# Head attention on one core: the product with the values moves to the second half of the next key tile

## The chip, the cores and the metric

One core of a Trainium2 chip runs the whole program in one launch. The metric is the device time of that launch in microseconds (us). The engines are TensorE (PE, with its weight loads listed as PEld), VectorE (DVE), ScalarE (ACT), GpSimd (POOL) and SyncE (SP, which issues most DMAs). Three runs of the kernel before took 1535.26, 1531.8 and 1535.34 us; the median is 1535.26.

## The reference, cut to what matters

Two layers, each an attention and a feed-forward part, over x (8 sequences x 256 x 512) and a context of the same shape. The first attention is the part that the change touches. It has 16 heads of 16 rows each; both axes of its score matrix, queries t and keys s, have 512 places:

```python
q = jnp.einsum('oc,bct->bot', Wq, target) + bq[None, :, None]
k = jnp.einsum('oc,bcs->bos', Wk, source) + bk[None, :, None]
v = jnp.einsum('oc,bcs->bos', Wv, source) + bv[None, :, None]
dot = jnp.einsum('bhdt,bhds->bhts', q, k) / math.sqrt(HEAD_DIM)
dot = mask * dot - (1.0 - mask) * NEG
amap = jax.nn.softmax(dot, axis=-1) * mask
out = jnp.einsum('bhts,bhds->bhdt', amap, v)      # heads joined again
x = x + out                                       # target was layernorm(x)
```

The rest (a feed-forward part whose weights are quantised and restored, a second attention with one head, a second feed-forward part with ternary weights) comes after it and isn't changed.

## The kernel before, in words

The program first restores quantised weights, then runs the head attention for 8 sequences (`head_attention_block`), then the dense rest. The head attention is a pipeline whose order is written out by hand, one queue for each engine; semaphores tie the queues together.

A sequence b is split into 4 groups g of 4 heads, a group into 4 key tiles c of 128 keys. A tile (g, c) has two halves of two heads. The scores are computed twice. `row_scores` (line 828, TensorE) has the queries on the partitions; VectorE takes each row's maximum from it (`maxima`, line 1162), 16 blocks for a group, ahead of the group's turn. `column_scores` (line 837) has the keys on the partitions and the maximum already subtracted, through three extra rows of the stacked operand Qs. ScalarE takes its exponential (`exps`, line 920) into `prob`. Row scores use three PSUM banks in turn (pA), column scores three others (pB): a row matmul waits until the maximum of the third one before it is taken, a column matmul until the exponential of the third one before it is taken.

`values` (line 847, TensorE) multiplies `prob` of one key tile with the values of four heads, four products of 32 columns beside each other, and adds up over the 4 key tiles in the bank pV. It waits for the last exponential of its tile, and for its first tile of a group also until pV has been read. `av_evac` (line 925, ScalarE) copies pV to U. Before the change `values` of a tile stands behind the first half of the next tile, and `av_evac` behind the first two exponentials of tile (g, 0).

Between them the table `MISC` puts side jobs, all of which use the single bank pM, so that each waits until the one before has been read. For a tile it names a job behind the first and one behind the second half: q and k of the next sequence (line 782; in (0,0) and (1,0), q in the first half, k in the second), v of the next sequence (line 788; two in (2,3)), nm, which turns the split row maxima of the next group (line 801; first half of (g,1)), t, which turns U back (line 795; first half of (g,2)), and o, which turns the finished sequence before (line 817; two in (0,3)). Where a job and `values` stand in the same half, `values` is first.

Their readers: ScalarE reads q and k (`q_evac`, line 903) and nm (`nm_evac`, line 913); GpSimd then splits q and k into three bfloat16 parts (`split`, from line 990) and issues the DMA that puts the maxima into Qs (`max_rows`, line 1022). VectorE reads t (`normalise`, lines 1191 to 1198, behind the first two maxima of (g, 2)), v (line 1183) and o (`residual`, line 1207), which adds the input x that SyncE has loaded to xres (line 716). VectorE also splits the maxima (`max_parts`, lines 1170 to 1176, behind the last maxima of (g, 0)), takes statistics for the normalised input (`ln_stats`, behind (1,3)), a peak of the context (behind (2,1)) and applies the normalisation (`ln_apply`, line 1148, behind (3,2)).

SyncE stores the parts of q and k to memory and fills the stacks Qs and Ks from there (`fill`, lines 688 to 695), each group once the column matmuls that read it are through; the fill of group 3 is the last thing that it does for a sequence, and the load of xres is the first of the next.

The row matmuls that run beside the columns of a tile belong to a group ahead: in tile (g, 0) the last four blocks of group g + 1, in the other tiles the first twelve of group g + 2. In the last sequence there are no q, k and v jobs, and the row matmuls end with tile (2,0).

Of the kernel before, what the change touches and what calls it, by code (L numbers as in the profile page):

```python
# [59 lines left out]
def wait(eng, sem, value):  # L60

    if isinstance(value, int) and value <= 0:
        return
    eng.wait_ge(sem, value)
# [433 lines left out]
def head_attention_block(nc, keep, dram, A):  # L498
# [3 lines left out]
    with ExitStack() as ctx:  # L502
# [115 lines left out]
        def present(job, first, last):  # L618
            return job is not None and not (job[2] < 0 and first) and not (job[2] > 0 and last)

        def row_units(b, g, c):

            ahead = g + 1 if c == 0 else g + 2
            nb, ng = (b, ahead) if ahead < NG else (b + 1, ahead - NG)
            return nb, ng, 12 if c == 0 else 4 * (c - 1), ahead >= NG
# [11 lines left out]
        def over_sequences(body):  # L637
            for b in range(B):
                body(b, b == 0, b == B - 1, b >= B - 2)
# [111 lines left out]
        def _(pe):  # L751
# [69 lines left out]
            def row_scores(b, g, u):  # L821

                if u == 0:
                    pe.wait_ge(filled[g], FILL * (b + 1))
                n = 64 * b + 16 * g + u
                wait(pe, s["max_done"], n - 2)
                j, tt = u // 4, u % 4
                nc.tensor.matmul(pA[n % 3], Qs[0:MAX_ROW, g, j, P * tt:P * (tt + 1)], Ks[0:MAX_ROW, g, j, :],  # L828
                                 start=True, stop=True).then_inc(s["a_pe"], 1)

            def column_scores(b, g, c, j):

                if c == 0 and j == 0:
                    pe.wait_ge(maxrow[g], 16 * (b + 1))
                n = 64 * b + 16 * g + 4 * c + j
                wait(pe, s["exp_done"], n - 2)
                nc.tensor.matmul(pB[n % 3], Ks[:, g, j, P * c:P * (c + 1)], Qs[:, g, j, :],  # L837
                                 start=True, stop=True).then_inc(s["b_pe"], 1)

            def values(b, g, c):  # L840

                pe.wait_ge(s["exp_done"], 64 * b + 16 * g + 4 * c + 4)
                if c == 0:
                    wait(pe, s["av_act"], 4 * b + g)
                    pe.wait_ge(s["vt_ready"], 4 * b + g + 1)
                for j in range(G):
                    x = nc.tensor.matmul(pV[32 * j:32 * (j + 1), :], vt[:, g % 2, c, j, :], prob[:, c, j, :],  # L847
                                         start=(c == 0), stop=(c == DK - 1))
                x.then_inc(s["av_pe"], 1)
# [15 lines left out]
            def body(b, first, last, ending):  # L865
                for g in range(NG):
                    for c in range(DK):

                        nb, ng, u0, next_one = row_units(b, g, c)
                        jobs = MISC.get((g, c), [None, None])  # L870
                        for half in range(2):
                            for j in (2 * half, 2 * half + 1):
                                column_scores(b, g, c, j)
                                if not (last and next_one):
                                    row_scores(nb, ng, u0 + j)
                            if half == 0:
                                if c:
                                    values(b, g, c - 1)
                                elif g:
                                    values(b, g - 1, DK - 1)  # L880
                                elif not first:
                                    values(b - 1, NG - 1, DK - 1)
                            if present(jobs[half], first, last):
                                kind, i, ahead = jobs[half]
                                run(kind, i, b + ahead)
                            if last and (g, c) in LAST and LAST[g, c][half]:
                                run(*LAST[g, c][half])

            over_sequences(body)
            values(B - 1, NG - 1, DK - 1)  # L890
            run("t", 3, B - 1)
# [3 lines left out]
        @block.scalar  # L895
        def _(act):
            def q_evac(b, i, which=(0, 1)):
                for n in which:
                    act.wait_ge(s["q_pe"], 4 * b + 2 * i + n + 1)
                    if n == 0:  # L900
                        act.wait_ge(s["bias"], 1)
                    wait(act, s["q_pool"], 4 * b + 2 * i + n - 1)
                    nc.scalar.activation(qf[n][:], pM[:], ACT.Identity, bias=(bq4 if n == 0 else bk)[:, i:i + 1],  # L903
                                         scale=0.25 if n == 0 else 1.0).then_inc(s["q_act"], 1)

            def nm_evac(b, g):
                act.wait_ge(s["nm_pe"], 4 * b + g + 1)

                if g >= 2:
                    act.wait_ge(maxrow[g - 2], 16 * (b + 1))  # L910
                else:
                    wait(act, maxrow[g + 2], 16 * b)
                nc.scalar.activation(nrow[g % 2][:], pM[0:3 * G, :], ACT.Copy).then_inc(s["nm_act"], 1)

            def exps(b, g, c, half):
                for j in (2 * half, 2 * half + 1):
                    act.wait_ge(s["b_pe"], 64 * b + 16 * g + 4 * c + j + 1)
                    if j == 0:
                        wait(act, s["av_pe"], 16 * b + 4 * (g - 1) + c + 1)
                    nc.scalar.activation(prob[:, c, j, :], pB[(64 * b + 16 * g + 4 * c + j) % 3], ACT.Exp).then_inc(s["exp_done"], 1)  # L920

            def av_evac(b, g):
                act.wait_ge(s["av_pe"], 16 * b + 4 * g + 4)
                wait(act, s["t_pe"], 4 * b + g)
                nc.scalar.activation(U[:], pV[:], ACT.Copy).then_inc(s["av_act"], 1)

            for u in W["scalar"](act):
                if u - 1 in FIRST and FIRST[u - 1][0] in "qk":
                    kind, i, _ = FIRST[u - 1]
                    q_evac(0, i, ("qk".index(kind),))  # L930

            act.wait_ge(W["d_used"], W["d_steps"])
            act.wait_ge(W["a_used"], W["a_steps"])
            nm_evac(0, 0)

            def body(b, first, last, ending):
                for g in range(NG):
                    for c in range(DK):
                        exps(b, g, c, 0)
                        if c == 0:  # L940
                            if g:
                                av_evac(b, g - 1)
                            elif not first:
                                av_evac(b - 1, NG - 1)
                            if g < 2 and not last:
                                q_evac(b + 1, g, (0,))
                        if c == 1:
                            if g < NG - 1:
                                nm_evac(b, g + 1)
                            elif not last:  # L950
                                nm_evac(b + 1, 0)
                        exps(b, g, c, 1)
                        if c == 0 and g < 2 and not last:
                            q_evac(b + 1, g, (1,))
                        if last and (g, c) == (3, 0):
                            act.wait_ge(s["x_turned"], 1)
                            nc.scalar.activation(xh.rearrange("p k t -> p (k t)"), turned2.rearrange("p a b -> p (a b)"),
                                                 ACT.Copy, scale=XS).then_inc(s["x_high"], 1)

            over_sequences(body)  # L960
            av_evac(B - 1, NG - 1)

# [1078 lines left out]
```

## Time and profile before

| | us |
|---|---|
| median of three runs | 1535.26 |
| the profiled execution, its own time | 1524.93 |
| its span | 1523.1 |
| TensorE busy in it | 1390.8 |
| VectorE busy in it | 1031.6 |
| ScalarE busy in it | 592.7 |
| GpSimd busy in it | 276.1 |

Profile numbers come from the one profiled execution, not from the three runs. Busy shares are averages over stages with different limits. A matmul's listed duration contains the time to drain the array, so neighbouring matmuls overlap in the listing; the step from one start to the next says how fast they are issued.

### The profile page before, as it was taken

What the parts mean: (1) busy time and instruction counts of PE and PEld (TensorE: products, weight loads), DVE (VectorE), ACT (ScalarE), POOL (GpSimd) and SP (SyncE); (2) the same over time, 40 slices, a digit from 0 to 9 for tenths busy, and PEclk for the clock granted to TensorE, in tenths of its full rate; (3) what the DMA queues carried; (4) which work ended last, traced back from release to release, by engine and by line L of the source; (5) the groups of instructions that cost most, each with busy time, mean ns of one, the idle gap of its engine ahead of it and who ended that gap; (6) DMA issues with size and microseconds to landing.
All of it is one profiled execution on the core that took longest, in us unless ns stands there. A gap on an engine that the chain in (4) does not pass through costs nothing.

```text
span 1523.1 us, 23289 instructions
## 1 busy us (share of the span) xinstructions
PE 1390.8 (91%) x8981; PEld 811.0 (53%) x9010; DVE 1031.6 (68%) x1826; ACT 592.7 (39%) x925; POOL 276.1 (18%) x495
## 2 busy tenths in 40 slices
PE   3799899899999999988898799899998999989998
PEld 1344333333333333322676577677776777767776
DVE  9987778878787887875795945654446535465353
ACT  4567366655665565555262111122111221112310
POOL 5014062533536263310000000000000000000000
PEclk9999899999999999999999999999999999999999
DMA  5012223333434333320743401000010000110000
GB/s 176 6 32 78 81 64 108 111 115 95 133 98 148 115 113 98 101 81 15 252 130 114 133 29 56 1 29 1 15 66 5 28 1 1 46 39 29 1 2 28
DMA packets 66466, 105.64 MB, mean 69 GB/s; under 512 B 13359, under 2 KB 38071, under 8 KB 66343
## 3 DMA queue, kind: packets, MB, share of 16 engines
q1 hardware_dynamic: 65335, 103.77, 21.6%
q8 instruction: 73, 1.20, 0.3%
q0 software_dynamic: 1024, 0.40, 0.1%
q14 instruction: 34, 0.28, 0.1%
HBM read 82.40 MB, written 21.35 MB: 68 GB/s over the span
## 4 chain that ended last, share of the span: by engine, by line
PE 34%; DVE 12%; DMA 4%; ACT 1%; issue 1%; POOL 0%; SPq 0%; DVEq 0%; POOLq 0%; ACTq 0%
PE double L1584 10%; PE double L1598 10%; PE double L1610 5%; PE double L1620 2%; PE double L1663 2%; PE double L1631 2%; DMA x_early<-scr_x 2%; DVE f1w L1920 1%; DMA out_x<-x_early 1%; PE double L1650 1%; DVE hid L1824 1%; DVE hv L1822 1%; DVE gate L1821 1%; PE double L1568 1%; ACT th L1708 1%
## 5 line engine op out<-in xcount | busy, mean ns | idle before, releaser
L1162 DVE TENSOR_REDUCE nmx<-level 128x1 f32<-128x512 f32 x512 | 320.1, 681 | 52.9 <-PE level L828 52.0
L920 ACT ACTIVATE prob<-level 128x512 f32<-128x512 f32 x512 | 267.7, 593 | 136.6 <-PE level L837 136.2
L828 PE MATMUL level<-Ks,Qs 105*128 105x512 bf16 x512 | 201.0, 395 | 21.3 <-DVE nmx L1162 20.1
L1708 ACT ACTIVATE th<-double 128x512 f32<-128x512 f32 x96 | 53.9, 562 | 414.1 <-PE double L1584 204.8
L837 PE MATMUL level<-Qs,Ks 108*128 108x512 bf16 x512 | 194.9, 384 | 1.0 <-ACT prob L920 0.8
L1584 PE MATMUL double<-x_parts,f0w 128*128 128x256 f16 x1408 | 157.1, 274 | 5.4 <-DVE hid L1824 2.5
L1584 PE MATMUL double<-x_parts,f1w 128*128 128x256 f16 x1408 | 155.0, 273 | 2.7 <-DVE x_parts L1809 2.7
L1584 PEld LDWEIGHTS double<-x_parts,f0w 128*128 128x128 bf16 x1408 | 137.8, 98 | 24.9 <-issue 3.9
L365 PE MATMUL level<-prob,x_parts 128*128 128x448 bf16 (+1 forms) x527 | 118.3, 378 | 33.4 <-ACT prob L317 15.2
L1584 PEld LDWEIGHTS double<-x_parts,f1w 128*128 128x128 bf16 x1408 | 137.6, 98 | 20.7 <-DVE x_parts L1809 3.1
L1770 POOL TENSOR_TENSOR rstd<-meanvar,halfpow 128x2 f32<-128x2 f32 x22 | 15.2, 691 | 725.9 <-DVE meanvar L1790 725.9
L847 PE MATMUL pV<-prob,vt 128*32 128x512 f32 x1024 | 137.2, 608 | 1.5 <-ACT prob L920 1.0
L828 PEld LDWEIGHTS level<-Ks,Qs 105*128 105x128 bf16 x512 | 50.3, 98 | 107.9 <-DVE nmx L1162 64.3
L365 PEld LDWEIGHTS level<-prob,x_parts 128*128 128x128 bf16 x540 | 53.0, 101 | 91.5 <-issue 23.9
L317 ACT ACTIVATE prob<-f1w,level_edge 128x1408 bf16<-128x1408 bf16 x60 | 85.5, 1461 | 36.9 <-PE level L365 36.8
L837 PEld LDWEIGHTS level<-Qs,Ks 108*128 108x128 bf16 x512 | 49.9, 98 | 89.2 <-ACT prob L920 37.3
L1598 PE MATMUL double<-f0w,hid 128*128 128x512 bf16 x344 | 82.1, 401 | 10.0 <-DVE hid L1824 9.7
L1598 PE MATMUL double<-f1w,hid 128*128 128x512 bf16 x344 | 75.6, 379 | 4.8 <-DVE hid L1831 4.6
L412 DVE TENSOR_SCALAR prob<-f1w 128x1408 bf16<-128x1408 bf16 x120 | 60.4, 560 | 19.5 <-PE level L365 19.2
L990 POOL TENSOR_TENSOR qf<-qf,mrow 128x512 f32<-128x512 f32 x32 | 40.5, 1266 | 151.4 <-ACT qf L903 151.4
L1598 PEld LDWEIGHTS double<-f0w,hid 128*128 128x128 f16 x352 | 35.6, 103 | 54.6 <-DVE hid L1824 9.9
L1829 DVE SCALAR_TENSOR_TENSOR gate<-th,double 128x512 f32<-128x512 f32 (+1 forms) x48 | 30.8, 642 | 42.3 <-ACT th L1708 42.3
(206 smaller groups left out, 1893.9 us busy)
## 6 DMA issues: line engine op xcount, KB each, us to landing
scr_q<-qp SPq DMA_DIRECT2D x16, 384.0 KB, 9.3
scr_k<-qp SPq DMA_DIRECT2D x16, 384.0 KB, 3.1
Qs<-scr_q SPq DMA_DIRECT2D x32, 192.0 KB
Ks<-scr_k SPq DMA_DIRECT2D x32, 192.0 KB
hid<-in_f1w1t SPq DMA_DIRECT2D x8, 704.0 KB, 5.8
hid<-in_f1w2t SPq DMA_DIRECT2D x8, 704.0 KB, 4.2
xin<-in_x SPq DMA_DIRECT2D x8, 512.0 KB, 13.2
cx<-in_ctx SPq DMA_DIRECT2D x8, 512.0 KB, 13.7
```

The source lines that it names most:

```text
L317: nc.scalar.activation(sa[:, n % RING_A, :], wn[w][:, UNIT * q:UNIT * (q + 1)], ACT.Sign, bias=edge[:, j:j + 1]).then_inc(a_made, 1)
L365: x = nc.tensor.matmul(acc[u % 2][:, c, 0:m], diag[:, level, :], tile[:, c0:c0 + m], start=(at == 0), stop=(at == len(MIX) - 1))
L412: nc.vector.tensor_scalar(sd[:, n % RING_D, :], wn[w][:, UNIT * q:UNIT * (q + 1)], FROM[ON_DVE[j]], None, ALU.is_ge).then_inc(d_made, 1)
L828: nc.tensor.matmul(pA[n % 3], Qs[0:MAX_ROW, g, j, P * tt:P * (tt + 1)], Ks[0:MAX_ROW, g, j, :], start=True, stop=True).then_inc(s["a_pe"], 1)
L837: nc.tensor.matmul(pB[n % 3], Ks[:, g, j, P * c:P * (c + 1)], Qs[:, g, j, :], start=True, stop=True).then_inc(s["b_pe"], 1)
L847: x = nc.tensor.matmul(pV[32 * j:32 * (j + 1), :], vt[:, g % 2, c, j, :], prob[:, c, j, :], start=(c == 0), stop=(c == DK - 1))
L920: nc.scalar.activation(prob[:, c, j, :], pB[(64 * b + 16 * g + 4 * c + j) % 3], ACT.Exp).then_inc(s["exp_done"], 1)
L1162: nc.vector.tensor_reduce(nmx[:, g % 2, u // 4, u % 4:u % 4 + 1], pA[(64 * b + 16 * g + u) % 3], AX.X, ALU.max, negate=True).then_inc(s["m ...
L1584: y = nc.tensor.matmul(ps_[:, e, S * n:S * (n + 1)], w[n][:, k, P * (f0 + e):P * (f0 + e + 1)], part[:, k, :], start=(k == 0 and part is x ...
L1598: y = nc.tensor.matmul(ps_[:, t, :], hid[:, r, f, P * t:P * (t + 1)], w[:, f, :], start=(f == 0 and r == 0), stop=(f == FK - 1 and r == pa ...
L1610: y = nc.tensor.matmul(ps_[:, e // 2, (e % 2) * S:(e % 2 + 1) * S], wat[kind][:, r, k, P * e:P * (e + 1)], part[:, k, :], start=(k == 0 an ...
L1708: y = nc.scalar.activation(th[:, 0:m, :], src[:, 0:m, 0:S], ACT.Tanh, scale=0.5 / XS)
```

## The change

In TensorE's queue `values` moves from behind the first half of a tile to behind the second half; it still stands ahead of a side job of the same half. In ScalarE's queue `av_evac` moves from tile (g, 0) to tile (g, 1), behind the first two exponentials there and ahead of `nm_evac`; `q_evac` of q keeps its place.

```diff
@@ tensor
-                            if half == 0:
+                            if half == 1:
                                 if c:
                                     values(b, g, c - 1)
                                 elif g:
...
@@ scalar
                         exps(b, g, c, 0)
-                        if c == 0:
+                        if c == 0 and g < 2 and not last:
+                            q_evac(b + 1, g, (0,))
+                        if c == 1:
                             if g:
                                 av_evac(b, g - 1)
                             elif not first:
                                 av_evac(b - 1, NG - 1)
-                            if g < 2 and not last:
-                                q_evac(b + 1, g, (0,))
-                        if c == 1:
                             if g < NG - 1:
                                 nm_evac(b, g + 1)
                             elif not last:
```

## Rows read from the trace of the kernel before

**Rows 1.** The page: span, TensorE's busy time, and a load's time to landing.

```profile
span 1523.1 us, 23289 instructions
...
PE 1390.8 (91%) x8981; PEld 811.0 (53%) x9010; DVE 1031.6 (68%) x1826; ACT 592.7 (39%) x925; POOL 276.1 (18%) x495
...
x_early<-scr_x SPq DMA_DIRECT2D x8, 512.0 KB, 4.0
```

**Rows 2.** Busy time by stretch: from, to, length, engines, granted clock, DMA share, GB/s.

```profile
255.67:656.23 400.56, 374.59 (x1970) 138.51 (x1968) 324.10 (x641) 239.81 (x457) 175.28 (x323) 1.00 0.36 113
390.04:456.16 66.12, 62.52 (x329) 23.06 (x328) 54.34 (x109) 40.03 (x78) 29.33 (x54) 1.00 0.38 114
674.00:680.00 6.00, 5.70 (x19) 1.93 (x20) 3.52 (x7) 2.14 (x4) 0.00 (x0) 0.50 0.23 87
```

**Rows 3.** Waits by pair, 190 to 722 us: total, times, longest.

```profile
PEld level L828 <- DVE nmx L1162: 54.7, 83, 1.4
...
DVE xres L1207 <- DMA xres<-in_x: 14.2, 7, 5.3
```

**Rows 4.** TensorE's timeline in sequence 3: start, duration, line, idle before.

```profile
389.48 0.38 PE L837 MATMUL level<-Qs,Ks 108*128 108x512 bf16 x1
...
401.92 0.66 PE L795 MATMUL pM<-identf,U 128*128 128x128 f32 x4
...
404.98 0.39 PE L828 MATMUL level<-Ks,Qs 105*128 105x512 bf16 x1 [0.87 <-DVE nmx L1162]
405.30 1.07 PE L847 MATMUL pV<-prob,vt 128*32 128x512 f32 x8
406.30 0.66 PE L817 MATMUL pM<-identf,O 128*128 128x128 f32 x4
...
407.44 0.38 PE L828 MATMUL level<-Ks,Qs 105*128 105x512 bf16 x1
408.08 0.66 PE L817 MATMUL pM<-identf,O 128*128 128x128 f32 x4 [0.26 <-DVE xres L1207]
...
410.54 1.98 PE L782 MATMUL pM<-tgt,wq 128*128 128x512 f32 x4
```

**Rows 5.** The same timeline: nm in tile (1,1); first columns of (2,3) and (3,0).

```profile
416.09 1.06 PE L847 MATMUL pV<-prob,vt 128*32 128x512 f32 x8
416.97 0.39 PE L801 MATMUL pM<-identb,nmp 128*12 128x128 bf16 x4
417.29 0.39 PE L837 MATMUL level<-Qs,Ks 108*128 108x512 bf16 x1
...
435.99 0.38 PE L837 MATMUL level<-Qs,Ks 108*128 108x512 bf16 x1
...
443.51 0.38 PE L837 MATMUL level<-Qs,Ks 108*128 108x512 bf16 x1
```

**Rows 6.** SyncE's timeline, 380 to 425 us: first refill, and the load of xres.

```profile
389.89 0.72 SPq L688 DMA_DIRECT2D Qs<-scr_q  x1
...
394.77 0.40 SPq L716 DMA_DIRECT2D xres<-in_x  x1
```

**Rows 7.** The line that loads xres: seven loads, from issue to landing.

```profile
DMA to landing us min/median/max: 12.5/13.6/14.6
```

**Rows 8.** VectorE's timeline in sequence 3.

```profile
402.62 0.26 DVE L1191 RECIPROCAL rs<-pM 128x16 f32<-128x16 f32 x1 [0.41 <-PE pM L795]
...
404.25 2.47 DVE L1162 TENSOR_REDUCE nmx<-level 128x1 f32<-128x512 f32 x4
...
407.34 0.69 DVE L1207 TENSOR_TENSOR xres<-pM,xres 128x512 f32<-128x512 f32 x1 [0.62 <-DMA xres<-in_x]
...
428.01 2.48 DVE L1162 TENSOR_REDUCE nmx<-level 128x1 f32<-128x512 f32 x4
```

**Rows 9.** ScalarE's timeline in sequence 3: the evacuation of q.

```profile
412.56 0.69 ACT L903 ACTIVATE qf<-pM,bq 128x512 f32<-128x512 f32 x1 [1.29 <-PE pM L782]
```

**Rows 10.** TensorE's timeline: the last value product of sequence 7.

```profile
714.50 1.07 PE L847 MATMUL pV<-prob,vt 128*32 128x512 f32 x8 [0.96 <-ACT prob L920]
```

## The prediction

> **What bounds the kernel now.** I read the page first: TensorE is busy 91% of a span of 1523.1 us [rows 1]. That is an average, so next came the busy times by stretch [rows 2]. The change lies in a loop of eight sequences, 192 to 716 us; sequences 1 to 6 take 400.56 us together, 66.76 each, with TensorE busy for 374.59, VectorE 324.10, ScalarE 239.81, GpSimd 175.28. What follows 720 us is untouched. Then the waits by pair [rows 3]: TensorE's weight loads before row matmuls wait 54.7 us for VectorE's maxima, and the residual addition waits 14.2 us, in 7 waits, for the load of xres.
>
> I call a column matmul c, a row matmul r, the value product V, and a tile (g,c), (0,0) opening a sequence. In the timeline of sequence 3, c and r start 0.22 us apart when nothing waits. V starts 0.31 after the r ahead of it and the next job 1.00 later: 1.09 us more than without V [rows 4]. In (0,3) the second r waits 0.87 us for a maximum and V stands right behind it; (1,3) and (2,3) have the same pattern, with 0.85 and 0.72.
>
> **One wait ties a sequence to the next.** SyncE refills Qs and Ks once the last column matmul of a sequence (c3 of (3,3), 389.48) has ended, from 389.89; only behind the eight refills, at 394.77, comes the load of xres, with 12.5/13.6/14.6 us to landing [rows 4, 6, 7]. The residual addition of (0,3) starts as it lands (407.34, 0.69 us), and the second transpose of O, o1 (408.08), waits for it [rows 4, 8]. So c3 to o1 takes 5.3 + 12.5 + 0.8 = 18.6 us here, and 5.1 + 13.6 + 0.8 = 19.5 in the mean (5.1: in sequence 1 the issue comes 4.9 after c3). TensorE alone would reach o1 after 18.3 (last r 407.44, plus 0.3, from 389.48). The period is (o1 to the next c3) + max(19.5, TensorE's way from c3 to o1). Now: 408.08 to the opening of sequence 4 at 456.16 [rows 2, 4] is 48.08, less 0.57 from c3 to the opening, 47.5; plus 19.5 is 67.0.
>
> **The change part by part.** Nothing is added or removed; 128 V and 32 evacuations of U move in their queues. I laid the new order out tile by tile with these steps: a row is readable 0.42 after r's start, a maximum occupies VectorE 0.60, r(n+3) starts 0.73 after maximum n (404.25 to 404.98), t is readable 0.70 after its start (401.92 to 402.62) [rows 4, 8].
>
> *V behind c3 r3 instead of r1.* V now gives VectorE its 1.09 us after every four r. In (1,2) the normalisation starts 1.9 after the tile's start and takes 1.63 (402.62 to 404.25), to 3.53; the tile is 3.40 long. So in (1,3) VectorE does r2, r3 of the tile before from 0.13 and 0.73; the second r waits for 0.86 instead of 0.65, the rest not at all: 3.37 us for 3.87. (2,3), from 435.99 to 443.51 = 7.52 [rows 5], becomes 4 x 0.22, 0.09 + 1.83 for v0, 4 x 0.22, 1.09, 1.83: 6.6, as its wait falls under V.
>
> *Switches.* In 12 of 16 tiles V shared its switch with the job behind it (t, nm, q, o0, v0); in four others k, o1 or v1 now follow V. A job behind an r pays up to what V pays, 0.31 - 0.22 = 0.09; nm also pays 0.10 to get back to c (0.32 for 0.22 of work), which V to nm (0.88 against 1.00) used to save [rows 4, 5]. r to t and r to nm aren't in the trace: bounds 0 and 0.19, I take 0.09 as the row nearest in kind. 8 x 0.09 + 4 x 0.10 = 1.1 us a sequence, contained in the lengths below.
> The skill speaks against the change here. In the trace the 98 ns weight loads of c and r are wholly hidden in 0.22 us steps [rows 4]. The Trainium skill, page "TensorE: Matmul & The Clock Gate", section "The mechanism", lets a weight load overlap running matmuls only where the row group differs; all of these share their rows, so the trace disagrees. By that rule every separated job would pay its load whole and the sum would lose some 0.2 us a sequence, 1.5 in all.
>
> *New waits.* (0,1), (1,1): nm comes 1.09 earlier and waits for the evacuation of k (2.0 after k's start, as 410.54 to 412.56 for q, plus 0.69 [rows 4, 9]), and V waits for that of U, which stands behind it and two exponentials: 0.1 and 0.25. With the switches 3.55 for 3.05. (1,0): o1 to q is 1.43 of work, but the second residual needs two maxima and itself after the first, 1.87: o1 to (1,1) 7.47 for 7.04. (2,0): VectorE's statistics end 2.04 after its start (in (2,0) of this sequence they end at 428.01 [rows 8]); the fourth r waits until 2.77 for its 1.53: 4.07 for 3.61. (2,1): nm, due at 0.96, waits 0.27 for the split maxima, but the backlog is gone: 3.51 for 3.69. (3,0) 2.92 for 2.85; (3,1) 3.46 for 3.23, nm 0.24 late. (3,3): normalisation and ln_apply (0.91) leave VectorE at the first row of (3,3) only 4.87 after the start of (3,2), so r3 comes at 5.60 instead of 4.93: 3.50 for 3.24. (0,0) 6.54 for 6.87. Tiles with t 3.40 for 3.33.
> On ScalarE the evacuations of U and nm are now neighbours; behind them stand two exponentials whose banks TensorE needs only 1 us later. GpSimd gets q 1.1 us sooner and then waits for nm as before; SyncE's order is the same.
>
> *The tie.* Behind the last c3 now stand r3 (waiting 0.67), V and then the opening: 2.19 us for 0.57. Refill and xres start 1.62 us earlier against the opening. TensorE's way from c3 to o1 is 2.19 + 6.54 + 3.56 + 3.40 + 3.60 = 19.3, the transfer's 19.5; as landings spread over 2.1 us, the larger of the two is 19.7 in the mean, +0.2.
>
> *Sum.* o1 to c3: 7.47 + 3.55 + 3.40 + 3.37 + 4.07 + 3.51 + 3.40 + 6.63 + 2.92 + 3.46 + 3.40 + 3.50 - 2.19 = 46.5 for 47.5; with +0.2, -0.8 a sequence. Sequences 1 to 5: -4.0. Sequence 6 has no statistics and no ln_apply: -0.6. Sequence 0 has no o: +0.4 of waits and switches, less 1.6 by c3: -1.2. Sequence 7, short of q and k, is held longest by the landing (5.3 [rows 3]); its idle stretch shrinks from 4.9 to about 3.1. After it the granted clock is 0.50, the lower level, from 674 to 680 [rows 2], and the tile there takes 5.3 for a usual 2.85; I count half of that back, -1.2. Its last six tiles have no r and go from exponential to V to exponential (V waits 0.96 for one at 714.50 [rows 10]); with V behind c3 the exponentials run under it, -0.25 a tile, -1.5. In all -8.5 us. The profiled execution (1524.93) becomes 1516.4; the median of the runs shown is 10.3 above it, 1535.26, so 1526.8.
>
> **Rivals.**
> 1. *The tie eats it: no change.* If the way from c3 to o1 is 0.6 longer than laid out (nm for k, V for U), each sequence gives back what it won; sequences 0 and 7 leave -1 to -4: 1531 to 1535. For it: 19.3 against 19.5 is a hair. Against: the waits won behind o1 don't hang on it.
> 2. *More than forecast.* If nm and q don't wait (1.2 us a sequence: 0.44 in (1,0), 0.25 twice, 0.5 in (2,1), (3,1)) and the clock stays up in sequence 7: -8.5 - 7 x 1.2 - 1.2 = -18: 1517. Against: four maxima of 0.60 outlast four pairs of 0.44.
> 3. *The landing doesn't follow its trigger: slower.* A load of the size of xres takes 4.0 us elsewhere [rows 1] and 13.6 here, behind the refills, so it should move with them. But if the traffic that holds it stays in place (stores of q and k, the x1 store), the 1.62 is lost: the gate is 21.1 after c3, 1.4 above what I count, so +0.6 a sequence, +4 in six, and sequence 7 +1.6, with its longer low clock another +1; with sequence 0 and the tail 1539. It decides once issue to landing exceeds 14.4 in the mean. Against: 12.5 to 14.6 in seven loads.
>
> **How the numbers follow.** Forecast 0.49, rival 1 0.28, rival 2 0.08, rival 3 0.15. A measurement of this kernel can't tell less than 0.3%, 4.6 us, from no change. Faster 0.57, same 0.28, slower 0.15. The forecast's own range is 1521 to 1530: switches at their bounds are 0.7 a sequence either way, the clock 1.2. For 8 in 10 I take in rival 1 and the near sides of 2 and 3: 1518 to 1538.
>
> **What would show it.** Right: the second r of (1,3) and (2,3) hardly waits; last c3 to opening grows from 0.57 to about 2.2; the waits for xres fall from 14.2 to under 9; o1 to (0,0) stays near 48.7 while the period of sequences 1 to 5 is near 66.2; (2,0) about 4.1. Wrong: issue to landing above 14.4; the 54.7 us not below 45; waits for the evacuation of U or k above 0.5 each.

## The result and the profile after

| | before | changed |
|---|---|---|
| median, us | 1534.2 (4 runs, 1531.8 to 1535.34) | 1517.76 (4 runs, 1515.08 to 1521.58) |
| ratio, 95% interval | | 0.9911 (0.9894 to 0.9928) |
| profiled execution: span | 1523.1 | 1513.3 |
| first column matmul of the loop to the first dense matmul | 529.54 | 515.59 |

The ratio makes 13.7 us (11.0 to 16.3) of 1534.2; the two medians differ by 16.4. The two profiled executions differ by less, 9.8, because the changed one reached the loop 2.8 us later (195.05 for 192.28) and spent 1.3 more behind it, both outside the change; the loop itself (from its first column matmul to the first dense matmul) is 13.95 us shorter, which agrees with the ratio. So in what follows I compare stretches inside the loop, each of one execution. The forecast was -8.5 with 1526.8 us; the measured median is 0.2 below the low end of the range, 1518.

The busy times of sequences 1 to 6 together, of sequence 3, and of a stretch of sequence 7, in the changed kernel (from, to, length, PE, PEld, DVE, ACT, POOL, granted clock, DMA share, GB/s):

```profile
258.76:647.21 388.45, 371.95 (x1973) 137.84 (x1969) 321.62 (x640) 239.55 (x456) 176.22 (x323) 1.00 0.37 116
388.54:453.33 64.79, 62.02 (x333) 22.98 (x329) 54.01 (x109) 39.93 (x76) 29.47 (x54) 1.00 0.37 116
664.20:669.50 5.30, 5.26 (x16) 2.12 (x20) 4.64 (x7) 2.39 (x4) 0.00 (x0) 0.50 0.26 99
```

Against [rows 2] the busy times hardly differ (371.95 for 374.59 on TensorE); what is gone is idle time: 388.45 us for 400.56. The low clock in sequence 7 is still there.

Its waits by pair, 190 to 712 us (total, times, longest), answering to [rows 3]:

```profile
PEld level L837 <- ACT prob L920: 65.6, 81, 1.1
...
PEld level L828 <- DVE nmx L1161: 39.0, 76, 1.6
...
PE pM L801 <- DVE nmp L1175: 5.7, 16, 0.7
...
DVE xres L1206 <- DMA xres<-in_x: 7.2, 5, 4.7
```

The wait for maxima before row matmuls, counted at their weight loads, fell from 54.7 to 39.0 (the matmuls themselves sat idle 9.6 us for 19.7), that for xres from 14.2 to 7.2, 4.7 of it in sequence 7. A new one is nm waiting for the split maxima, 5.7 us. (The wait before column weight loads grew from 37.3 to 65.6 us, but it is idle time of the weight loader; the matmuls themselves sat idle 1.1 us behind it, as the page lists.)

TensorE's timeline in sequence 3, from the last column matmul of sequence 2 (386.30) on, answering to [rows 4, 5]:

```profile
386.30 0.38 PE L837 MATMUL level<-Qs,Ks 108*128 108x512 bf16 x1
387.23 0.39 PE L828 MATMUL level<-Ks,Qs 105*128 105x512 bf16 x1 [0.55 <-DVE nmx L1161]
387.54 1.06 PE L847 MATMUL pV<-prob,vt 128*32 128x512 f32 x8
388.54 0.39 PE L837 MATMUL level<-Qs,Ks 108*128 108x512 bf16 x1
...
399.04 0.38 PE L828 MATMUL level<-Ks,Qs 105*128 105x512 bf16 x1
399.26 0.60 PE L795 MATMUL pM<-identf,U 128*128 128x128 f32 x4
399.69 0.38 PE L837 MATMUL level<-Qs,Ks 108*128 108x512 bf16 x1
...
402.43 0.39 PE L828 MATMUL level<-Ks,Qs 105*128 105x512 bf16 x1
402.65 0.60 PE L817 MATMUL pM<-identf,O 128*128 128x128 f32 x4
...
404.06 1.06 PE L847 MATMUL pV<-prob,vt 128*32 128x512 f32 x8
405.05 0.66 PE L817 MATMUL pM<-identf,O 128*128 128x128 f32 x4
...
425.17 0.39 PE L828 MATMUL level<-Ks,Qs 105*128 105x512 bf16 x1 [1.05 <-DVE nmx L1161]
...
427.15 0.38 PE L828 MATMUL level<-Ks,Qs 105*128 105x512 bf16 x1
427.88 0.38 PE L801 MATMUL pM<-identb,nmp 128*12 128x128 bf16 x4 [0.35 <-DVE nmp L1175]
428.20 0.39 PE L837 MATMUL level<-Qs,Ks 108*128 108x512 bf16 x1
```

What to see: the second r of (0,3) comes at 402.43, 0.1 late, where 0.87 stood. From the last c3 to the opening are 2.24 us. t starts 0.22 behind an r, the same step as between any two matmuls, and c follows 0.43 later. In (2,0) the fourth row waits 1.05, and nm of (2,1) 0.35. The xres loads of the changed kernel, issue to landing, for [rows 7]:

```profile
DMA to landing us min/median/max: 12.6/13.1/14.2
```

I put the start of c3, of the load of xres, its landing, and of o1 of every sequence beside each other. Means of sequences 1 to 5, us:

| | before | changed | forecast |
|---|---|---|---|
| o1 to the next last column matmul (c3) | 47.51 | 46.05 | 46.5 |
| c3 to the issue of xres | 5.01 | 5.02 | 5.1 |
| issue to landing | 13.73 | 13.34 | 13.6 |
| landing to o1 | 0.77 | 0.78 | 0.8 |
| c3 to o1 | 19.51 | 19.14 | 19.7 |
| sum, the period | 67.02 | 65.19 | 66.2 |

Median tile lengths of sequences 1 to 5, groups (g) down, before and changed: (0,c) 6.87 3.05 3.33 6.22 and 6.38 3.45 3.28 4.01; (1,c) 6.54 3.05 3.33 3.87 and 6.90 3.45 3.29 3.26; (2,c) 3.61 3.69 3.33 7.52 and 4.07 3.69 3.28 6.40; (3,c) 2.85 3.23 3.33 3.24 and 2.93 3.69 3.28 3.56.

### The profile page after: what moved, and what is told of

It is laid out like the page before. It is cut to its first block, busy times and chain, and to the rows that moved or that the text cites. A ratio compares the mean times of both kernels' runs of the same rounds, so it can differ in the third digit from the quotient of the medians.

```text
span 1513.3 us, 23289 instructions
## 1 busy us (share of the span) xinstructions
PE 1392.0 (92%) x8981; PEld 812.7 (54%) x9010; DVE 1030.0 (68%) x1826; ACT 592.8 (39%) x925; POOL 277.2 (18%) x495
## 4 chain that ended last, share of the span: by engine, by line
PE 34%; DVE 12%; DMA 3%; ACT 2%; issue 1%; POOL 1%; SPq 0%; DVEq 0%; POOLq 0%; ACTq 0%
PE double L1583 11%; PE double L1597 10%; PE double L1609 5%; PE double L1662 2%; PE double L1619 2%; PE double L1630 2%; DMA x_early<-scr_x 1%; DMA out_x<-x_early 1%; PE double L1649 1%; DVE hid L1823 1%; DVE f1w L1919 1%; DVE hv L1821 1%; DVE gate L1820 1%; PE double L1567 1%; ACT th L1707 1%
## 5 line engine op out<-in xcount | busy, mean ns | idle before, releaser
L920 ACT ACTIVATE prob<-level 128x512 f32<-128x512 f32 x512 | 273.7, 594 | 145.7 <-PE level L837 144.1
L828 PE MATMUL level<-Ks,Qs 105*128 105x512 bf16 x512 | 200.9, 394 | 10.3 <-DVE nmx L1161 10.2
L837 PEld LDWEIGHTS level<-Qs,Ks 108*128 108x128 bf16 x512 | 49.6, 98 | 128.2 <-ACT prob L920 65.6
L1597 PEld LDWEIGHTS double<-f0w,hid 128*128 128x128 f16 x352 | 35.7, 103 | 55.1 <-issue 10.2
## 6 DMA issues: line engine op xcount, KB each, us to landing
xin<-in_x SPq DMA_DIRECT2D x8, 512.0 KB, 13.6
cx<-in_ctx SPq DMA_DIRECT2D x8, 512.0 KB, 13.2
```

Source lines behind the costliest of these rows:

```text
L1597: y = nc.tensor.matmul(ps_[:, t, :], hid[:, r, f, P * t:P * (t + 1)], w[:, f, :], start=(f == 0 and r == 0), stop=(f == FK - 1 and r == pa ...
```

## Experiments

Four kernels ran first, to find which part of the move carries the gain; all ratios are against the kernel before, run beside them.

**V moved in (3,3) alone.**

```diff
-                            if half == 0:
+                            if half == (1 if (g, c) == (3, 3) else 0):
                                 if c:
```

> The kernel before, with V in the second half of tile (3,3) alone; all other tiles and ScalarE's order as before. Theory 1 (V is cheap where TensorE waits for the load of xres anyway): V leaves the stretch from o1 to the last column matmul, 47.5 to 46.4 us, and enters the one from there to o1, where it fills a wait of 1.2: 19.5 to about 19.7. That is -0.9 in each of six sequences, -1.1 in sequence 0, -1 in sequence 7, some of it lost in the tail: about -7 us against the kernel before. Theory 2 (the gain is VectorE's waits in (g,3) falling under V): those waits of 0.87, 0.85 and 0.72 stay, so within 1.5 us of the kernel before.

Measured: 0.9999 (0.9986 to 1.0011), 1528.85 us beside 1530.37: nothing. Theory 1 would have 7 us, theory 2 at most 1.5. The stretches say why neither is the whole. o1 to c3 did fall, to 46.6 (-0.9), as theory 1 has it. But c3 to o1 rose to 20.6 in the mean of sequences 1 to 5. TensorE's timeline of this kernel, sequence 2 into 3:

```profile
390.92 0.38 PE L837 MATMUL level<-Qs,Ks 108*128 108x512 bf16 x1
392.20 0.39 PE L828 MATMUL level<-Ks,Qs 105*128 105x512 bf16 x1 [0.90 <-DVE nmx L1162]
392.52 1.07 PE L847 MATMUL pV<-prob,vt 128*32 128x512 f32 x8
393.52 0.39 PE L837 MATMUL level<-Qs,Ks 108*128 108x512 bf16 x1
```

In (3,3) VectorE is behind (normalisation, ln_apply), and taking V out of its first half makes the last row wait 0.90; from c3 to the opening are 2.6 us, where I had counted 1.66. TensorE's own way to o1 is then 20.05 (sequences 2 and 3, in which o1 was not held by the load), longer than the load needed before. The loads also took longer, 13.2/14.2/15.8, for a reason that I can't name. Of the rise by 1.04, TensorE's own way is about half and the slower loads the rest.

**V moved in every tile but (3,3).** The changed kernel with

```diff
-                            if half == 1:
+                            if half == (0 if (g, c) == (3, 3) else 1):
                                 if c:
```

> The changed kernel, with V of tile (3,3) alone back in the first half. Theory 1: the stretch from the last column matmul to o1 is again ruled by the load (19.1 to 19.5) with TensorE early, the one from o1 to it grows from 46.05 to 47.1: +6 to +7 us against the changed kernel, -6 to -7 against the kernel before. Theory 2: the gain stays, -12 to -14 against the kernel before.

Measured: 0.9992 (0.9973 to 1.0012), 1528.09 us: again nothing, where theory 1 has -6 to -7 and theory 2 -12 to -14. The traced execution is the fastest of the ten, 7.2 below their median. Measured alone, each part of the move is worth nothing, and both together are worth 13.7. The stretches again: o1 to c3 is 47.15 in sequences 1 and 2 (forecast 47.1), and c3 to o1 19.3 although TensorE could be there after 17 (16.91 in the kernel of this order without the load's wait, below). It waits for the load, up to 3.2 us, and three of these waits had a second cost. Its timeline in sequence 4, then the busy times from 474.6 (the clock is the number after POOL):

```profile
474.11 0.66 PE L817 MATMUL pM<-identf,O 128*128 128x128 f32 x4 [3.23 <-DVE xres L1206]
...
475.06 0.63 PE L837 MATMUL level<-Qs,Ks 108*128 108x512 bf16 x1
475.16 0.68 DVE L1206 TENSOR_TENSOR xres<-pM,xres 128x512 f32<-128x512 f32 x1
475.49 0.63 PE L828 MATMUL level<-Ks,Qs 105*128 105x512 bf16 x1
475.76 1.28 DVE L1161 TENSOR_REDUCE nmx<-level 128x1 f32<-128x512 f32 x2
475.91 3.20 PE L782 MATMUL pM<-tgt,wq 128*128 128x512 f32 x4
```

```profile
474.60:479.00 4.40, 4.40 (x11) 1.67 (x9) 2.44 (x5) 1.19 (x2) 0.00 (x0) 0.61 0.11 41
```

Behind the idle stretch the clock fell to its lower level: a matmul is listed with 0.63 instead of 0.38, q with 3.20 instead of 1.98. Sequences 3 to 5 lose 1.2 to 1.6 us each that way in (1,0), and the ten runs spread from 1520.9 to 1535.1. The length of the idle stretch doesn't decide it: in sequence 3 the clock fell behind 1.58 us, in sequence 2 it stayed up behind 2.48. The granted clock from 2.4 us before o1 to 3.6 behind it in sequence 2, and in the 6 us behind o1 in sequence 3:

```profile
337.00:343.00 6.00, 3.34 (x12) 1.56 (x13) 3.68 (x6) 1.09 (x2) 0.28 (x1) 1.00 0.26 93
405.00:411.00 6.00, 5.60 (x16) 2.40 (x16) 3.10 (x7) 1.56 (x3) 0.00 (x0) 0.72 0.25 76
```

**The load ahead of the refill, V as before, and V as changed.** The same edit of SyncE's queue in both kernels (the load moves from the start of a sequence to the end of the one before, ahead of the last refill):

```diff
-                if not first:
-                    wait(sp, s["out_store"], 16 * b)
-                    sp.dma_start(xres[:], x_t[b - 1]).then_inc(s["xr_in"], 16)
...
                 if not last:
+                    sp.wait_ge(s["out_store"], 16 * (b + 1))
+                    sp.dma_start(xres[:], x_t[b]).then_inc(s["xr_in"], 16)
                     fill(b + 1, 3)
```

> The kernel before, with the load of xres issued ahead of the refill of group 3 instead of behind it; V where it was. Both theories: no wait for xres is left, the stretch from the last column matmul to o1 is TensorE's own, 18.3 for 19.5, -1.2 in six sequences; in sequence 7 the idle 4.9 us go and the clock stays at the higher level, another -2.5: -14 us against the kernel before.

> The changed kernel with the same early load. Theory 1: V behind the last column matmul is no longer free, so the change is worth less here: 18.75 for 19.14 to o1 in six sequences and 4.1 + 2.5 in sequence 7, about -9 against the changed kernel, and about -8 against the kernel before with the early load (o1 to last column -1.5, last column to o1 +0.5, seven times). Theory 2: the change keeps its whole 14 us: -14 against the kernel before with the early load.

Measured: with V as before 0.9919 (0.9902 to 0.9937), 1516.33 us, near the -14 expected (-12.4). With V as changed 0.9837 (0.9818 to 0.9856), 1504.57 us: -12.5 against the former by the ratios, -10.4 in the loop (517.56 to 507.16). Against the changed kernel it is -11.3 by the ratios and -8.4 in the loop (515.59 to 507.16), where -9 was expected. Without the load's wait, c3 to o1 is TensorE's own way: 18.32 with V as before, 18.75 as changed. o1 to c3 is 47.50 and 45.82 (here and below for the early load, the usual value of sequences 1 to 5; sequence 4 stands apart). So the move is worth 1.25 us a sequence where no load is in the way; theory 1's -8 is 2.4 short by the loop's figure and theory 2's -14 is 3.6 too much. In sequence 7, (0,3) fell from 9.57 to 4.23 us and (1,0) from 5.32 to 2.85 with the early load and V as before: the wait and its low clock. The early load has a price, too. In sequence 4, where SyncE issues two more loads (x2), o1 to c3 is 1.8 us longer than in its neighbours with V as before (49.30) and 0.9 as changed (46.74). TensorE stands there for maxima and refills that land late; with V as before:

```profile
490.78 0.61 PE L836 MATMUL level<-Qs,Ks 108*128 108x512 bf16 x1 [1.99 <-DMA Qs<-nrow]
```

**All but (3,3), with the early load.** 

> The changed kernel with V of (3,3) in the first half and the early load. If the period is the sum of what TensorE needs once the load is out of the way, it is 47.15 (o1 to last column) + 17.1 (0.44 + 6.37 + 3.45 + 3.29 + 3.4): 64.2 for 64.56, so -1 to -3 us against the changed kernel with the early load, though with the late load the same step cost +12. If V behind the last column is worth something by itself, it is slower than that kernel by 5 or more.

This is the changed kernel with the early load and the one-line edit of the kernel with V moved in every tile but (3,3). Measured: 0.9818 (0.9788 to 0.9847), 1502.73 us; the loop 502.90 for 507.16. With the load out of the way this kernel has 46.92 + 16.91 = 63.83 us a period, the changed one 45.82 + 18.75 = 64.57, before 47.50 + 18.32 = 65.82. The periods and the loop came out as the sum says, -0.7 in each sequence (loop -4.3); the whole runs don't tell the two apart (medians -1.8, with intervals that overlap). So V in the second half of (3,3) is no gain by itself. It is a gain of 12 by the ratios (10.2 in the loops, 525.79 to 515.59) only with the late load: there it turns a wait for the load, which the rest of the move had opened, into work, and shortens the stretch ahead of the load's trigger. 4.2 of the 10.2 are the low clock in sequences 3 to 5, which the changed kernel doesn't have.

**V moved in (g,2) and (3,3) alone**, the places where VectorE is behind; with the late and with the early load:

```diff
-                            if half == 0:
+                            if half == (1 if c == 2 or (g, c) == (3, 3) else 0):
                                 if c:
```

> The kernel before (ScalarE's order too), with V in the second half of the tiles (g,2) and of (3,3) alone. If V's worth lies in the two places where VectorE is behind (after a normalisation, after ln_apply), and the rest of the move costs (nm that waits in (2,1), (3,1), (0,1), (1,1); the fourth row in (2,0)), the stretch from o1 to the last column matmul is about 44 us (46.05 in the changed kernel, 47.5 before) and the one back to o1 19.2: period 63.2, -25 us against the kernel before, -11 against the changed one. Rival: V is needed behind every four rows; then waits come up elsewhere and it is no better than the changed kernel, -14.

> The same with the load of xres issued ahead of the refill of group 3. The load's wait goes (0.8 in each of six sequences, 6 to 7 in sequence 7 with its low clock): about -35 us against the kernel before. Under the rival -26, as the changed kernel with the early load.

Measured: 0.9971 (0.9953 to 0.9989), 1524.59 us, and 0.9909 (0.9881 to 0.9937), 1516.53, so -4.4 and -13.9: the rival was right in kind, and even its -14 and -26 were too much. TensorE's timeline of the former, a V of (1,1), then of (1,2) and (1,3), with the t between:

```profile
416.55 1.06 PE L847 MATMUL pV<-prob,vt 128*32 128x512 f32 x8
...
419.51 0.60 PE L795 MATMUL pM<-identf,U 128*128 128x128 f32 x4
...
420.91 1.06 PE L847 MATMUL pV<-prob,vt 128*32 128x512 f32 x8
...
423.61 0.39 PE L828 MATMUL level<-Ks,Qs 105*128 105x512 bf16 x1 [0.88 <-DVE nmx L1162]
423.93 1.07 PE L847 MATMUL pV<-prob,vt 128*32 128x512 f32 x8
```

Between the first two V stand six rows, between the next two only two. V behind six rows comes while VectorE has not caught up enough for the two that follow, and the 0.88 in (1,3) is back (3.90 for 3.87); (2,2) grew to 4.15. The whole move keeps four rows between V everywhere, with the normalisation ahead of V instead of behind it.

**Statistics and ln_apply elsewhere.** The changed kernel with the early load, and

```diff
+                            if (g, c, half) == (1, 0, 0) and not ending:
+                                ln_stats(b + 2)
+                            if (g, c, half) == (2, 3, 0) and not ending:
+                                ln_apply(b + 2)
                             if g == 2 and c == 3 and not last:
                                 v_evac(b + 1, half)
-                        if g == 1 and c == 3 and not ending:
-                            ln_stats(b + 2)
...
-                        if g == 3 and c == 2 and not ending:
-                            ln_apply(b + 2)
```

with the load of xin three sequences ahead, behind the early load of xres.

> The changed kernel with the early load, and VectorE's statistics moved from behind (1,3) into (1,0), ln_apply from behind (3,2) into (2,3), where VectorE waits for q and v; the load of xin is issued a sequence earlier for it. If the 1.2 us in (2,0) and the 0.7 in (3,3) come from these two, both go: (2,0) 4.07 to 2.9, (3,3) 3.56 to 2.9: -1.9 in each sequence, -11 against the changed kernel with the early load, -36 against the kernel before. Rival: VectorE's total load rules, and the waits turn up in (1,1) and (3,0): within 3 us of the changed kernel with the early load.

Measured: 0.9788 (0.9758 to 0.9817), 1496.6 us, the fastest of all and ahead of both kernels. (2,0) fell from 4.07 to 2.84, (3,3) from 3.56 to 2.85, and nothing rose. Sequence period 62.5 for 64.57; the loop 495.21 for 507.16, -12. So these two waits were the ones named, and in the changed kernel they cost 2 us a sequence. The waits of row weight loads for maxima, in this kernel and then in the changed one with the early load alone:

```profile
PEld level L829 <- DVE nmx L1162: 23.3, 72, 0.5
```

```profile
PEld level L827 <- DVE nmx L1160: 35.7, 71, 1.5
```

**nm in the second half of (2,1) and (3,1)**, on top of that kernel (ScalarE's `nm_evac` moves behind the tile's last two exponentials with it):

```diff
-            (2, 1): [("nm", 3, 0), None], ...
-            (3, 1): [("nm", 0, 1), None], ...
+            (2, 1): [None, ("nm", 3, 0)], ...
+            (3, 1): [None, ("nm", 0, 1)], ...
```

> The kernel with the early load and the moved statistics and ln_apply, and in tiles (2,1) and (3,1) the job nm in the second half, behind V, its evacuation behind the last two exponentials of the tile. If the 3.69 us of these tiles (3.28 for a tile with t) come from nm waiting for the split maxima, both fall to about 3.2 and nothing else changes: -0.9 a sequence, -5 to -6 us against the kernel without this step. Rival: t, half a tile behind, then waits for the evacuation of nm, or the maxima land late for (0,0): within 1.5 us.

Measured: 0.9799 (0.9764 to 0.9835), 1498.14 us: 1.5 above the kernel without it by the medians, which the intervals don't tell from nothing, where -5 to -6 was expected; the loop is 3.9 longer (499.11 for 495.21). (2,1) fell from 3.56 in that kernel (not 3.69, as I had it) to 3.30 and (3,1) from 3.69 to 3.43, so nm had waited for the split maxima. But column matmuls now wait more for the maxima to land, 10.7 us for 4.0, counted at their weight loads, and the rival's second half holds; 2.7 of the loop's 3.9 are in sequence 4 alone.

```profile
PEld level L838 <- DMA Qs<-nrow: 10.7, 8, 2.1
```

**The load of xres later, behind that of xin.**

```diff
+                if not ending:
+                    load_x(b + 2)
                 if not first:
                     wait(sp, s["out_store"], 16 * b)
                     sp.dma_start(xres[:], x_t[b - 1]).then_inc(s["xr_in"], 16)
...
-                if not ending:
-                    load_x(b + 2)
```

> The changed kernel with the load of xin (512 KB) issued ahead of that of xres instead of behind it; all else as in the changed kernel. If the load's landing ties each sequence to the next, xres comes 0.5 us later into the queue and lands some 4 to 5 us later (13.3 us now for 0.85 MB of refills and 0.5 MB of its own), and every sequence from 1 to 6 grows by that, and by 1 to 1.5 more where TensorE's idle stretch lets its clock fall: +30 to +40 us against the changed kernel. If the tie isn't what holds the sequences (or transfers of one queue run beside each other), the change is under 10 us.

Measured: 0.9991 (0.9968 to 1.0014), 1528.9 us: the whole gain is gone, +12 us against the changed kernel. Direction as the tie has it, size a third. Two rows tell why: from issue to landing the loads take only 1.6 us more by the median (13.1 in the changed kernel), where 4 to 5 was expected, so transfers don't stand strictly behind each other; and the matmuls behind o1 run with the clock down (0.57 granted from 414.4 to 418.4).

```profile
DMA to landing us min/median/max: 12.6/14.7/15.3
```

```profile
414.35 0.66 PE L817 MATMUL pM<-identf,O 128*128 128x128 f32 x4 [2.22 <-DVE xres L1206]
414.84 0.59 PE L837 MATMUL level<-Qs,Ks 108*128 108x512 bf16 x1
...
415.65 0.63 PE L837 MATMUL level<-Qs,Ks 108*128 108x512 bf16 x1
...
416.51 2.77 PE L782 MATMUL pM<-tgt,wq 128*128 128x512 f32 x4
```

In sequences 1 to 5 c3 to o1 is 21.02 (+1.9) and o1 to c3 47.20 (+1.15, all in (1,0), the clock). Sequence 6, which loads no xin, is as in the changed kernel: 18.73.

## Why the prediction was right, and where its size was off

*What bounds the loop.* Right: the max of TensorE's way and the load. (The issue follows c3 by 5.01 in the mean, not 5.1; nothing hangs on it.) It is what made each part of the move worthless and the whole worth 14, with the slower loads and the low clock named above taking their share in the parts: with the late load c3 to o1 is 19.5 with V as before, 20.6 with V moved in (3,3) alone, 19.3 in all but (3,3), 19.1 as changed; without the load 18.3, 18.75 and 16.9 (the second of the four wasn't run so).

*V behind c3 r3.* Right: (1,3) 3.26 for 3.37 laid out, (2,3) 6.40 for 6.6; the 0.87 of (0,3) is 0.1.

*Switches: the step that failed in size.* I took 1.1 us a sequence. A job behind an r costs nothing: 399.04 to 399.26 for t, 402.43 to 402.65 for o0; the same 0.22 holds for v and for q. So the weight loads stayed hidden at these places too, and the 1.5 us that the prediction put on paying them whole didn't come. The job is even shorter than behind V, t 0.43 for 0.49. Only nm pays, 0.09 and 0.10. A tile with t went from 3.33 to 3.28 where I had 3.40, (0,0) to 6.38 where I had 6.54, (2,3) to 6.40 where I had 6.63. The price of a change of kind sat on the side of V, not of the job. Over the four tiles with t, (0,0) and (2,3) this is 0.9 us a sequence, about 6 in seven.

*New waits.* In place and about in size: nm and V in (0,1), (1,1) 3.45 (3.56, 3.55 laid out), the fourth row in (2,0) 4.07 (4.07), nm in (2,1), (3,1) 3.69 (3.51, 3.46: here 0.2 short), (3,3) 3.56 (3.50). The experiment with statistics and ln_apply moved shows the causes of (2,0) and (3,3); the one with nm later shows that of (2,1) and (3,1).

*The tie.* 2.24 us from c3 to the opening for 2.19. TensorE's way was 18.75, not 19.3 (switches, and o1's row 0.1 late instead of 0.2), and the loads 0.39 faster than before instead of equal. So c3 to o1 fell by 0.37 where I had +0.2. The faster loads are about half of it, which is chance as far as is known; no run shows whether the change made them faster: they took 12.6 to 14.2 here, 13.2 to 15.8 with V moved in (3,3) alone.

*The sum.* Term by term, forecast and measured in the loops of the two traces: sequence 0 (opening to c3) -1.2, -1.35; sequences 1 to 5 -4.0, -9.15; sequence 6 -0.6, -2.4 (the same errors, and without statistics and ln_apply (2,0) and (3,3) keep none of the new waits); sequence 7 and the tail -2.7, -1.1. Together -8.5, -14.0. In sequence 7 I had counted half of the low clock back: it stayed, (1,0) 5.34 for 5.32, with an idle stretch that shrank to 4.0, not 3.1. That overestimate of 1.6 there hid part of what the other terms fell short by, 7.1. Its last tiles won 1.7, and 0.6 of that went again as the last V of two now stand behind each other (c3 to dense 9.25 for 8.67).

*Signs.* All that spoke for right came but one: the period is 65.19, not near 66.2. Of those for wrong none came: 13.3 from issue to landing, and 54.7 us down to 39.0.

*Rivals.* 1 (the tie eats it) asked for a way 0.6 longer than laid out; it was 0.5 shorter. The experiments show how near it was: with V moved in (3,3) alone TensorE's way was 20.05 and nothing was gained, and with the load behind that of xin the landing and the low clock took all of it back. 2 had nearly the right total (1517), for a wrong reason: nm and q still wait, and the clock still falls (and its own terms add up to 1.4 us a sequence, not 1.2). 3 (the landing keeps its place) failed: the issue follows c3 by 5.0, and the landing follows the issue by 13.3, no more than before.

## What to carry to other kernels

Where a transfer triggered at the end of one round is waited for in the next, the period is a sum of two stretches, one of them a maximum; work moved across the trigger, and work saved ahead of the wait, may each be worth nothing and together a lot, so a part of a change measured alone doesn't tell its share. Look first whether the load can be issued earlier: here that alone was worth nearly as much as the change (12.4 us), and both together with VectorE's long steps moved to where it waits for TensorE's f32 jobs 32.6. When work is spread for the engine that follows, keep the spacing even: the move of a few V to the places that waited made new ones.

## What the runs showed of the hardware

A wait of TensorE for a transfer could cost more than its length, and the length didn't tell whether it would. Behind idle stretches of 2.0 to 2.7 us the clock fell to the lower level in each of the sequences 1 to 5 of the kernel with the later load, for a loss of 1.2 us each in the mean. But with V moved in every tile but (3,3) it fell behind 1.58 us in sequence 3 and not behind 2.48 in sequence 2, and in the kernel before not behind 1.94.

A job of another kind behind a plain bf16 matmul started at the plain 0.22 us step, f32 transposes and f32 matmuls of 512 and 256 columns alike, while the value product started 0.09 later than that; behind the value product a column matmul came after 1.00, where nm came after 0.88.

A load of 512 KB put ahead of xres in the queue delayed its landing by 1.9 us (0.4 of it issue), though a load of that size takes 13 us from issue to landing there.
